# The first tile's down projection: its second half cast partly into the ring buffers, and three neighbouring orders of loads, stores and statistics changed

## What is computed

```python
xn = _layernorm(x)
x5 = tanh((xn + delta * x0_mu) @ x0_w.T)          # delta = shifted xn - xn
mix = einsum(x5, x2_w) + x_bias                   # five mixes: r, w, k, v, g
r, k, v, g = ((xn + delta * mu) @ w.T for each)   # r, k: 512 wide; v, g: 1024
o = chunk_rwkv6(r, k, v, w, bonus)                # state 128 x 256 for each of 4 heads
s = (group_norm(o) * silu(g)) @ o_w.T
h = silu(xn @ w_gate.T / 127) * (xn @ w_up.T / 127)   # 3072 wide
out = x + s * silu(h @ w_down.T / 127)
```

## Time and profile before

| | |
|---|---|
| median of 3 runs | 1734.38 us (1733.5 to 1734.84) |
| the profiled execution's own time | 1731.29 us |
| span of its slowest core (core 1) | 1729.7 us |
| spans of the eight cores | 1709.1 to 1729.7 us |
| granted TensorE clock, die 0 and die 1 | 0.989 and 0.996 of full speed |
| PE busy on core 1 | 1674.3 us, 97% of the span |
| DVE, ACT, POOL busy | 63%, 28%, 11% |
| DMA | 303.47 MB, 175 GB/s in the mean |

### The profile page before, as it was taken

How to read it: one execution, slowest core, us unless ns; L and a number is a source line. 1 busy time by engine, 2 the same in 40 slices (tenths; PEclk the granted TensorE clock), 3 DMA queues, 4 the chain that set the end, 5 groups by cost and what they waited for, 6 DMA issues and landing times.

```text
span 1729.7 us, 26524 instructions; the slowest of 8 cores (1709.1 to 1729.7 us)
## 1 busy us (share of the span) xinstructions
PE 1674.3 (97%) x9248; PEld 779.7 (45%) x9248; DVE 1087.2 (63%) x1844; ACT 480.7 (28%) x806; POOL 195.3 (11%) x408
## 2 busy tenths in 40 slices
PE   5999799999999999999999999999999999999998
PEld 2444344445444454344544445444454445544454
DVE  5565655656757476564875647757476485764856
ACT  1143211333114321143211432114321143212421
POOL 3112301112011020110200001000110001100000
PEclk9999899999999999999999999999999999999999
DMA  8999899997699777998436974465734355354422
GB/s 164 177 169 177 203 237 160 155 196 210 140 172 181 212 220 176 192 195 266 171 105 168 219 270 153 126 191 151 264 122 165 128 179 211 117 183 146 177 65 107
DMA packets 79234, 303.47 MB, mean 175 GB/s; under 512 B 10687, under 2 KB 15232, under 8 KB 73728
## 3 DMA queue, kind: packets, MB, share of 16 engines
q0 software_dynamic: 27456, 95.08, 34.2%
q10 hardware_dynamic: 25344, 124.79, 20.5%
q1 hardware_dynamic: 26304, 81.90, 13.7%
HBM read 348.56 MB, written 44.04 MB: 227 GB/s over the span
## 4 chain that ended last, share of the span: by engine, by line
PE 82%; DMA 11%; DVE 3%; issue 1%; DVEq 1%; POOL 1%; SPq 0%; ACT 0%; POOLq 0%; ACTq 0%
PE PB L1240 17%; PE PB L1245 16%; PE PB L1365 8%; PE PB L1354 7%; PE PB L1505 7%; PE PB L1528 6%; PE PB L1397 6%; DMA sb_gu<-w_gu 3%; PE PB L1450 3%; PE PB L1466 3%; DMA sb_wd<-kept_wd 3%; DMA sb_gu<-kept_gu 2%; DMA sb_wd<-w_fd 1%; DMA kept_gu<-sb_gu 1%; PE PB L1273 1%
## 5 line engine op out<-in xcount | busy, mean ns | idle before, releaser
L1240 PE MATMUL PB<-sb_xnT,sb_gu 128*128 128x512 bf16 x1536 | 366.2, 381 | 14.6 <-DMA sb_gu<-w_gu 5.9
L1245 PE MATMUL PB<-sb_xnT,sb_gu 128*128 128x512 bf16 x1536 | 364.3, 380 | 0.0
L920 DVE SCALAR_TENSOR_TENSOR sb_xin<-PB,sb_xb,sb_dT 128x512 bf16<-128x512 f32 x320 | 218.1, 744 | 172.8 <-PE PB L1273 172.7
L691 ACT ACTIVATE sb_scr<-PB 128x512 bf16<-128x512 f32 x192 | 113.8, 597 | 529.8 <-PE PB L1245 510.0
L1245 PEld LDWEIGHTS PB<-sb_xnT,sb_gu 128*128 128x128 bf16 x1536 | 150.8, 98 | 182.7 <-issue 3.3
L1240 PEld LDWEIGHTS PB<-sb_xnT,sb_gu 128*128 128x128 bf16 x1536 | 140.7, 98 | 201.8 <-issue 57.2
L852 DVE SCALAR_TENSOR_TENSOR sb_hall<-PB,sb_scr 128x512 bf16<-128x512 f32 x192 | 130.8, 685 | 125.7 <-ACT sb_scr L691 125.7
L1365 PE MATMUL PB<-sb_wd,sb_hall 128*128 128x512 bf16 x768 | 178.6, 381 | 10.0 <-DMA sb_wd<-w_fd 5.2
L1354 PE MATMUL PB<-sb_wd,sb_hall 128*128 128x512 bf16 x768 | 179.4, 383 | 6.6 <-DMA sb_wd<-w_fd 6.0
L459 POOL DMA_DIRECT2D sb_gu<-w_gu x106 | 57.5, 543 | 619.0 <-PE PB L1245 539.9
L700 ACT ACTIVATE sb_wc<-PB 128x512 bf16<-128x512 f32 x64 | 38.2, 597 | 316.2 <-PE PB L1365 316.2
(11 more groups left out here) (155 smaller groups left out, 1683.7 us busy)
## 6 DMA issues: line engine op xcount, KB each, us to landing
sb_gu<-w_gu POOLq DMA_DIRECT2D x106, 512.0 KB, 10.4
sb_gu<-kept_gu ACTq DMA_DIRECT2D x86, 512.0 KB, 5.3
sb_wd<-kept_wd ACTq DMA_DIRECT2D x56, 768.0 KB, 7.4
sb_ring<-kept_ring ACTq DMA_DIRECT2D x34, 1024.0 KB, 6.7
sb_xin<-x SPq DMA_DIRECT2D x48, 512.0 KB, 8.3
kept_gu<-sb_gu SPq DMA_DIRECT2D x24, 512.0 KB, 9.0
sb_ring<-w_g POOLq DMA_DIRECT2D x20, 512.0 KB, 13.8
sb_ring<-w_v POOLq DMA_DIRECT2D x16, 512.0 KB, 14.0
```

The lines of the kernel that those rows point to most:

```text
L691: e.activation(out=sb_scr[:, p, :], in_=GB[p][:], func=AF.Silu, bias=0.0, scale=INV127).then_inc(a_silu, 1)
L920: e.scalar_tensor_tensor(out=sb_xin[:, p, c, :], in0=PM[j][:], scalar=sb_xb[:, n, c:c + 1], in1=sb_dT[:, c, :], op0=ALU.add, op1=ALU.mult) ...
L1240: e.matmul(GB[p][:], sb_gu[:, sl, 0, c, :], sb_xnT[:, c, :], start=(c == 0), stop=(c == NC - 1))
L1245: i = e.matmul(UB[p][:], sb_gu[:, sl, 1, c, :], sb_xnT[:, c, :], start=(c == 0), stop=(c == NC - 1))
```

## The change

In tile 0, parts 0 and 1 of w_down's second half are cast into ring slots 0 and 1, as soon as the products of g have read them; parts 2 and 3 go to the places of parts 0 and 1 in `sb_wd`. Each half has its own semaphores. POOL issues the first four casts before the second part of the tile and the other four where all eight were. The casts of r and k for tile 1 now wait until u = 7 has read its first two parts and those are stored. In group t = 2 of tile 0, PE does the output projection of group 0 between the two halves of unit 4.

```diff
+    def wd_place(it, half, g):
+        if it or not half:
+            return sb_wd[:, 6 * g:6 * g + 6, :]
+        if g < 2:
+            return sb_ring[:, g, 0:6, :]
+        return sb_wd[:, 6 * g - 12:6 * g - 6, :]
...
+            if it:
                 return
-            e.wait_ge(d_wd[g], 32 * wd_counts(it, half, g)[0])
-            e.dma_start(kept_wd[half, g], sb_wd[:, 6 * g:6 * g + 6, :]
-                        ).then_inc(k_wd[g], 16)
+            e.wait_ge(d_wd[half][g], 32)
+            e.dma_start(kept_wd[half, g], wd_place(it, half, g)
+                        ).then_inc(k_wd[half][g], 16)
...
+            keep_gu(it, 4)
+            keep_gu(it, 5)
             replicate_x5(it, IR)
             replicate_x5(it, IK)
             replicate_x5(it, IV)
-            for hc in range(4, 9):
+            for hc in range(6, 9):
                 keep_gu(it, hc)
...
                 keep_wd(it, 0, g)
             if nxt:
                 load_x(it + 1, 3)
+            keep_wd(it, 1, 0)
+            keep_wd(it, 1, 1)
...
             store_out(it, 0)
-            for g in range(4):
-                keep_wd(it, 1, g)
+            keep_wd(it, 1, 2)
+            keep_wd(it, 1, 3)
             store_out(it, 1)
...
-            if j < 2 and it:
+            if j < 2 and it == 1:
+                e.wait_ge(t_wd, 4 + j)
+                e.wait_ge(k_wd[1][j], 16)
+            elif j < 2 and it:
                 e.wait_ge(t_g, 8 * it - 4 + 4 * j)
...
+        def cast_wd(half, g, p):
+            dst = wd_place(0, half, g)
+            if half and not p:
+                if g < 2:
+                    e.wait_ge(t_g, 4 + 4 * g)
                 else:
-                    e.wait_ge(t_D, 4 * k)
-            kept = wd_counts(it, half, g)[2] - (it == LAST_CAST_WD[half][g])
-            if kept:
-                e.wait_ge(k_wd[g], 16 * kept)
-            e.dma_start(sb_wd[:, c0:c0 + 3, :],
-                        wdr["w_fd"][half, :, c0:c0 + 3, :],
-                        max_dma_last_dim=8192).then_inc(d_wd[g], 16)
+                    e.wait_ge(t_wd, g - 1)
+                    e.wait_ge(k_wd[0][g - 2], 16)
+            e.dma_start(dst[:, 3 * p:3 * p + 3, :],
+                        wdr["w_fd"][half, :, 6 * g + 3 * p:6 * g + 3 * p + 3, :],
+                        max_dma_last_dim=8192).then_inc(d_wd[half][g], 16)
...
-            if it == 0:
-                e.wait_ge(v_lbn, n + 1)
+            if it == 0 and j % 2 == 0:
+                e.wait_ge(v_lbn, j // 2 + 1)
...
-            e.wait_ge(a_stat, n - 3)
-            e.wait_ge(v_xnt, n - 3)
+            stats = n - 1 if it else j // 2 + 1
+            e.wait_ge(a_stat, stats)
+            if it:
+                e.wait_ge(v_xnt, n - 3)
...
@@ -623,18 +623,22 @@
                 if it:
                     for hc in range(4):
                         cast_gu(it + 1, hc)
+                else:
+                    for g in range(2):
+                        cast_wd(1, g, 0)
+                        cast_wd(1, g, 1)
             for t in range(NST):
                 if nxt and t < 3:
                     ln_rstd(it + 1, t + 1)
                 gn_rstd(it, t)
-                if t == 1:
-                    for g in range(4):
-                        cast_wd(it, 1, g, 0)
-                        cast_wd(it, 1, g, 1)
+                if t == 1 and it == 0:
+                    for g in range(2, 4):
+                        cast_wd(1, g, 0)
+                        cast_wd(1, g, 1)
                 if t == 2 and it == 0:
                     for hc in range(4):
                         cast_gu(1, hc)
-                if t == 2 and nxt:
+                if t == (2 if it else 3) and nxt:
                     for j in (0, 1):
                         cast_ring(it + 1, j, 0)
                         cast_ring(it + 1, j, 1)
...
         def load_wd(it, half, g):
-            if it >= N_MT or it <= LAST_CAST_WD[half][g]:
+            if it == 0:
                 return
             k = 2 * it + half
-            if g < 3:
+            if k == 2 and g < 2:
+                e.wait_ge(t_D, 8)
+                e.wait_ge(k_wd[1][g + 2], 16)
+            elif g < 3:
                 e.wait_ge(t_wd, 3 * (k - 1) + g + 1)
             if it <= LAST_CAST + 1:
-                e.wait_ge(k_wd[g], 16 * wd_counts(it, half, g)[2])
+                e.wait_ge(k_wd[half][g], 16)
             e.dma_start(sb_wd[:, 6 * g:6 * g + 6, :], kept_wd[half, g]
                         ).then_inc(l_wd[g], 16)
 
         def ln_stat(it, j):
             n = 4 * it + j
-            src = x_ln[j % 2]
-            e.wait_ge(d_x[j % 2], 16 * (n // 2))
-            e.wait_ge(p_ln, n - 3)
-            e.wait_ge(v_h, NHC * it)
+            if it:
+                src = x_ln[j % 2]
+                e.wait_ge(d_x[j % 2], 16 * (n // 2))
+                e.wait_ge(p_ln, n - 3)
+                e.wait_ge(v_h, NHC * it)
+            else:
+                src = x_first[j]
+                e.wait_ge(d_x[1] if j == 1 else d_xp[1], 16)
```

ACT, DVE and PE:

```diff
@@ -748,7 +759,10 @@
 
         e.wait_ge(p_init, 1)
         e.activation(out=sb_ls[:, 0, :], in_=sb_mh[:, 0:2], func=AF.Silu)
+        ln_stat(0, 1)
         for j in range(NST):
+            if j == 1:
+                ln_stat(0, 3)
             e.wait_ge(t_xn, j + 1)
             e.activation(out=sb_xnT[:, :, j * 128:(j + 1) * 128],
                          in_=P_first[j % 2].rearrange("p (c t) -> p c t", c=NC),
@@ -791,6 +805,7 @@
             load_ring(it, 5)
             for hc in range(14, 17):
                 silu_gu(it, hc)
+                load_wd(it, 0, hc - 14)
             decay_exps(it)
             for half in range(2):
                 for t in range(NST):
@@ -800,9 +815,8 @@
                     e.activation(out=sb_v[:, t, half * 512:half * 512 + 512],
                                  in_=PM[t][:], func=AF.Copy, bias=0.0, scale=1.0
                                  ).then_inc(a_v, 1)
-                load_wd(it, 0, 2 * half)
-                load_wd(it, 0, 2 * half + 1)
                 if half == 0:
+                    load_wd(it, 0, 3)
                     silu_gu(it, 17)
                     silu_gu(it, 18)
             for hc in range(19, 24):
...
@@ -1129,13 +1143,10 @@
                           "p a b -> p (a b)")).then_inc(v_lbn, 1)
 
         first_stat(0)
-        first_stat(1)
         ln_xnt(0, 0)
         first_stat(2)
-        ln_xnt(0, 1)
-        first_stat(3)
-        ln_xnt(0, 2)
-        ln_xnt(0, 3)
+        for j in range(1, NST):
+            ln_xnt(0, j)
         shift_and_xin0(0)
         make_h(0, 0)
         make_h(0, 1)
...
@@ -1352,7 +1365,7 @@
                 if hc % 6 == 0 and t == 0:
                     wait_wd(it, half, hc // 6)
                 i = e.matmul(PB[u % 2][:], sb_hall[:, hc, 128 * t:128 * t + 128],
-                             sb_wd[:, hc, :], start=(hc == 0), stop=False,
+                             wd_col(it, half, hc), start=(hc == 0), stop=False,
                              skip_group_check=True)
                 if t == 3 and hc % 6 == 5:
...
@@ -1536,6 +1550,15 @@
                     xn_transpose(it + 1, t)
                 if t < 3:
                     scores(it, t + 1)
+                if it == 0 and t == 2:
+                    down_first(0, 4)
+                    og_transpose(0, 0)
+                    ks_transpose(0, 3)
+                    out_proj(0, 0)
+                    down_second(0, 4)
+                    down_first(0, 5)
+                    down_second(0, 5)
+                    continue
                 down_first(it, 2 * t)
                 if t >= 2:
                     og_transpose(it, t - 2)
```

More of the change, by code:

```diff
@@ L112 @@
 LAST_CAST_RING = [3, 3, 3, 3, 4, 4, 1, 1]
-LAST_CAST_WD = [[0, 0, 0, 0], [0, 0, 0, 0]]
 LAST_CAST = 5
@@ L139, in ring_counts @@
                   for h in range(j % 4, 8, 4) if (i, h) <= (it, j)])
-def wd_counts(it, half, g):
-    return tally([(i, LAST_CAST_WD[h][g]) for i in range(it + 1)
-                  for h in range(2) if (i, h) <= (it, half)])
 def build_program():
@@ L263, in build_program @@
     d_ring = [S("d_ring%d" % i) for i in range(4)]
-    d_wd = [S("d_wd%d" % i) for i in range(4)]
+    d_wd = [[S("d_wd%d%d" % (h, i)) for i in range(4)] for h in range(2)]
     l_gu = [S("l_gu%d" % i) for i in range(NGU)]
@@ L269, in build_program @@
     k_ring = [S("k_ring%d" % i) for i in range(4)]
-    k_wd = [S("k_wd%d" % i) for i in range(4)]
+    k_wd = [[S("k_wd%d%d" % (h, i)) for i in range(4)] for h in range(2)]
     (a_stat, a_x5, a_silu, a_h1, a_q, a_k, a_we, a_exE, a_exI, a_exS, a_dd,
@@ L526, in ln_rstd @@
                             ).then_inc(p_mean, 1)
-            e.wait_ge(p_mean, n - 3)
+            e.wait_ge(p_mean, stats)
             e.tensor_tensor(out=lr[:, 2:3], in0=lr[:, 0:1], in1=lr[:, 0:1],
                             op=ALU.mult).then_inc(p_msq, 1)
-            e.wait_ge(p_msq, n - 3)
+            e.wait_ge(p_msq, stats)
```

(20 more changed lines are left out.)

14 lines of the change are left out of this document (removed).

## The result

The changed kernel takes 1726.61 us (median of 5 runs) where the kernel before, beside it on the same chip, takes 1734.38. The ratio is 0.9946 with a 95% interval of 0.9928 to 0.9964, 0.54% faster (9.4 us; the medians differ by 7.8). The profiled execution took 1725.47 us (before: 1731.29).

What follows compares the result with a forecast made beforehand. PE was taken as the bound, busy 1674.3 of 1729.7 us. Gains of 8 + 1.7 + 2 = 11.7, rounded to 11.5, with 0 for the start, gave 1734.4 - 11.5 = 1723 us; range 1716 to 1731.

Steps and rivals of the forecast that it cites:

- part 1: Tile 0, w_down's second half cast earlier and PE's output projection between unit 4's halves: 8 us gained, bounds 3 and 14.8.
- part 2: SP stores block 4 before the replications, so a cast wait in tile 3 goes: 1.7 us gained, bounds 0 and 2.5.
- part 3: w_down's loads issued earlier: block 23's waits (5.9 us) go, block 18 loses 4.0; 2 us gained, bounds -3 and +6.
- part 4: At the start, ACT's passes for groups 1 and 3 put the first block 0.5 us later, covered by block 4's cast: 0.
- (a): Tile 0: x of group 2 lands near 188, so PE's transposition near 199 has a new wait of 2.2 us.
- (b): Tile 0: x of group 3, last in the store queue, lands near 203; ACT's copy follows at 206.6, `out_proj` runs to about 210.
- The bound of 4 us more: Tile 0: x of group 3 another 4 us late, with half clock until unit 5, leaves a gain of 3 us.
- (c): Tile 0: w_down's last cast part lands at about 214, unit 4 ends at 215.4 and unit 5 at 220.6.
- upper bound of 14.8: Tile 0 without any wait for transfers: unit 5 ends at 214.3 in place of 229.09, 14.8 us gained.
- room enough: Rival: stores give way and x is in time in tile 0, 13 us there, 20 in all, 1714.5 us; chance 0.2.
- The late x: Rival: tile 0's x of group 3 lands at 208, half clock, only 3 us gained there; total 1731 to 1734; chance 0.12.
- the slower case: Rival: w_down's loads pass ahead of block 18's casts in tiles 2 to 4; 9 us slower, 1743 us; chance 0.07.

Runs made afterwards that it cites:

- p3_only: The kernel before with only w_down's loads moved among the silus of blocks 14 to 16; ratio 1.0006 to the kernel before.
- after_again: The changed kernel itself, unaltered, run again on a second chip; ratio 0.9962 to the kernel before.
- a_swap: The changed kernel, but in tile 0 ACT copies group 0's transposed output ahead of the statistics of tile 1's group 3; ratio 0.9976 to the kernel before.
- a_x3: The changed kernel, but SP loads x of group 3 ahead of the stores of w_down's parts 2 and 3 (first half); ratio 0.9956 to the kernel before.
- a_late_swap: `a_swap` with four w_down stores moved out of tile 0's crowded stretch, behind store_out(0), and x of group 3 ahead of them; ratio 0.9966 to the kernel before.
- a_both_ends: `a_late_swap` with tile 1's r and k cast behind its block 4, and four w_down stores behind the replications for k; ratio 0.9981 to the kernel before.

## Why the prediction was right, and where its steps were not

The sign was right, and the total, 1726.6 against 1723, lies inside the range. The mechanism was right in kind: casts moved into idle time of the DMA engines. Its sizes were not, and that the total came so near is in part luck. In the end part 1 gave 2.8 us (0.7 to 4.7), part 2 3.5 to 5.0, part 3 about nothing (the interval of `p3_only` is -0.9 to +3.1 us of loss), part 4 nothing that can be seen, against 8, 1.7, 2 and 0. Part 2's surplus covered part of what part 1 lacked.

- **Part 1, (a)**: x of group 2 landed at 185.6 on core 4 (forecast 188), and the wait at the transposition was 0.91 us there and 0.7 to 2.7 on the eight cores of `after_again`. Right in size.
- **Part 1, (b)**: the term that was mis-sized. x of group 3 landed at 209.7 on core 4, 209.9 in the mean on the second chip, not 203. Two stores of the new parts (issued at 188.66 and 198.39 on core 4) ran beside x. They were counted in (c), where they lengthen the casts, but not in (b). The trace bears this out. The four x-sized loads (512 KB each) and four stores (768 KB) up to this x are 5.24 MB, and from 166 on the queue had moved 5.28 MB by 203, the forecast time. By 210, when x landed, it had moved 6.31 MB. So some 1.0 MB of the later stores went before the last of x. No run takes out these two stores alone. The bound of 4 us more was passed. The half clock for `out_proj` (6.35 us for 3.76) came on top.
- **Part 1, (c)**: the last cast part landed at 216.8 on core 4 (forecast 214), so even with x in time the gain would have been some 3 us less than 8. `a_swap` and `a_x3` show this term to be the one that sets the end.
- **The form of the sum** was wrong: PE's waits were added up as if each were PE's to gain. With the DMA engines 97% busy for 340 us, the gain of part 1 had another bound, the idle 4.6 us at 190 (0.92 x 5), and 2.8 were got. By this reading the upper bound of 14.8 and the case of room enough had no ground; `a_late_swap`, whose gain in tile 0 was gone by tile 2, supports it. Nothing waited for r, k or the early blocks in tile 1 of the kernel after, as forecast; in `a_late_swap` that cover failed at once, at block 4, for 2.5 to 6.5 us.
- **The late x**, a rival with a chance of 0.12, is what part 1 did (3 us, x at 208, half clock). The total, 7.8 us and not 4, differs from it mostly by what part 2 gave beyond its forecast.
- **Part 2**: right mechanism, one wait counted of three that stand behind one store.
- **Part 3**: block 23's waits went as forecast, and block 18 lost 5.9 us in the mean, not 4.0. With 6.3 us it passed the 6 us that were named as the sign of a wrong prediction, but what block 23 gave back paid for most of it. The place, block 18, was right, the 1.6 us of spare in tile 2 were not there: mean wait 3.4.
- **Part 4**: 1.6 us later, not 0.5 (22.8 and 24.4 in the mean in the first two profiles). Block 4's wait fell from 1.3 to 0.6 with it, so it took up 0.7, and no total shows the rest.
- **The Trainium skill's rule** that DMAs of all issuing engines share the same 16 ("DMA: Bandwidth & Descriptors", section "Issuing engines are not separate DMA queues") was used against the slower case alone. The trace agrees with it: the queues' shares add up to 103%, 96% and 103% in three windows. It should have bounded the gain of part 1 as well.

Left open: what makes the 0.81 stretches of one die, what part 2 gives beyond tile 3, and whether part 4 costs 1 us. Not tried: late stores with tile 1's first four casts issued before the statistics, so that the hole at 204 closes too.

## What to carry to other kernels

Before adding up the waits of the compute engine, take the DMA share over the stretch and well beyond it. Where it is as near to 1 as here (0.97 over 340 us), expect an earlier transfer to gain only the idle time that it fills, and the rest to come back as a wait further on, as it did in `a_late_swap` and `a_both_ends`. Whoever moves work out of such a stretch should first find one where the share is low, and look at which wait of another engine stands behind the moved transfers. A wait that several orders hide in turn (ACT's copy, then the last cast) is only seen by its next cover when the first is taken away, so a one-line swap is worth running before the sum is believed.

## What the hardware showed

- A megabyte of SP's queue has no fixed price in time of the DMA engines. With few casts beside it moved 5.23 MB in 82.5% of 18 us, 2.8 us per MB. Beside casts at equal packets it took 2.8, 2.95 (2.66 MB in 43.6% of 18 us), 2.7 (3.61 MB in 25.9% of 38 us, `a_both_ends`) and 3.5 (3.07 MB in 48.4% of 22 us, kernel after). What makes the last one dearer is not shown. By these prices the four stores of 0.79 MB that `a_late_swap` moved cost an estimated 8.5 to 11 us; the last cast came 9.4 us earlier, where 6 to 8 were expected.
- The split of two full queues is not fixed. Packets are equal (572 and 575, 614 and 611, 620 and 586), and the casts' share of the time was 68%, 59% and 47.5%. The shares follow what a packet costs on its engine: for a cast 0.38 us, 0.28 and 0.29, for SP's queue 0.19, 0.20 and 0.28 (share x window x 16 / packets). The 68% of (b) and (c) came from a window with dearer casts.
- A store issued behind others in such a stretch can take 28.7 us to land (an output store of 512 KB in `a_late_swap`, core 2, issued at 231.92), and DVE waited 11.31 us for it.
- The clock of one die went to 0.81 for four stretches of 15 us in one execution, 11 us in a span of 1730, while the other die had none, nor had any of the other profiles. That is more than the whole change.
